# A three-part edit to a mixture-of-experts megakernel: an earlier weight load, unwaited scatters, and spare rows cleared in other pieces

## What is computed

```python
x = x + _layernorm(_L0_attn_ref(_layernorm(x), ...))   # softmax attention, 16 heads of 16, causal
x = x + _layernorm(_L0_ffn_ref(_layernorm(x), ...))    # one 256x256 product
x = x + _layernorm(_L1_attn_ref(_layernorm(x), ...))   # linear attention, gelu feed-forward
x = x + _layernorm(_L1_ffn_ref(_layernorm(x), ...))    # 8 experts, top 2, capacity 2151
```

```python
probs = softmax(xf @ Wg); topv, topi = top_k(probs, 2); gates = topv / sum(topv)
pos   = running count of each expert's tokens; keep = pos < cap
buf   = zeros(e * cap + 1, d).at[dest].set(repeat(xf, 2))
h     = gelu(buf[e] @ W1[e] + b1[e]);  y = h @ W2[e] + b2[e]
out   = sum over a token's two experts of gate * y (0 where it was not kept)
```

## Time and profile before

| what | us |
|---|---|
| median of 3 runs (4597.26 to 4608.24) | 4602.2 |
| the profiled execution, its own time | 4610.1 |
| its span, first to last instruction | 4608.3 |
| softmax block, about | 0 to 1473 |
| linear block, about | 1473 to 3637 |
| experts block, about | 3637 to 4535 |
| combine block, about | 4535 to 4608 |

### The profile page before, as it was taken

How to read it: one execution, slowest core, us unless ns; L and a number is a source line. 1 busy time by engine, 2 the same in 40 slices (tenths; PEclk the granted TensorE clock), 3 DMA queues, 4 the chain that set the end, 5 groups by cost and what they waited for, 6 DMA issues and landing times. The chain is left out here.

```text
span 4608.3 us, 78285 instructions
## 1 busy us (share of the span) xinstructions
PE 4088.1 (89%) x26868; PEld 3115.5 (68%) x26868; DVE 2812.6 (61%) x8170; ACT 1910.7 (41%) x3047; POOL 1191.9 (26%) x1096
## 2 busy tenths in 40 slices
PE   4999999999993899999999999999999599989990
PEld 2344444444442788888888888888888498989890
DVE  4787777887862665555565655555655455556554
ACT  1565666666662333343243333332332233333322
POOL 3243333433422211111111111111111133333334
PEclk8899989999985999999999999999999699999995
DMA  3442443353322000000000000000000133333335
GB/s 71 84 88 54 76 100 55 73 112 76 54 51 90 4 17 14 19 19 15 14 15 16 15 13 13 15 13 4 13 13 9 62 60 63 64 61 67 61 65 200
DMA packets 168272, 222.45 MB, mean 48 GB/s; under 512 B 26732, under 2 KB 143435, under 8 KB 167872
## 3 DMA queue, kind: packets, MB, share of 16 engines
q1 hardware_dynamic: 139840, 180.74, 17.0%
q0 software_dynamic: 25728, 28.03, 4.0%
q10 hardware_dynamic: 2304, 8.39, 0.4%
HBM read 85.92 MB, written 86.65 MB: 37 GB/s over the span
## 5 line engine op out<-in xcount | busy, mean ns | idle before, releaser
L787 ACT ACTIVATE probs<-a_scores 128x1024 f32<-128x1024 f32 (+3 forms) x768 | 615.3, 811 | 376.9 <-PE a_scores L691 370.2
L948 DVE CUSTOM_DVE_ANT_0 a_scores<-a_scores,mask 128x384 f32<-128x384 f32 (+3 forms) x1024 | 482.1, 515 | 121.4 <-PE a_scores L677 115.4
L691 PEld LDWEIGHTS a_scores<-q_st,k_st 50*128 50x128 f32 x1536 | 151.4, 194 | 411.6 <-issue 282.0
L252 POOL TENSOR_TENSOR l_ln_rstd<-l_ln_ve,minus_half 128x4 f32<-128x4 f32 x80 | 84.0, 1050 | 1230.9 <-DVE l_ln_ve L225 1230.7
L691 PE MATMUL a_scores<-q_st,k_st 50*128 50x512 f32 (+3 forms) x1536 | 354.8, 460 | 33.5 <-issue 24.7
L951 DVE TENSOR_REDUCE mx<-a_scores 128x2 f32<-128x1024 f32 x256 | 311.0, 1224 | 118.0 <-PE a_scores L677 116.9
L711 PE MATMUL a_out<-probs,v_aug 128*32 128x512 f32 (+3 forms) x3072 | 352.1, 533 | 1.9 <-POOL probs L880 1.8
L677 PE MATMUL a_scores<-k_st,q_st 48*128 48x512 f32 (+3 forms) x1536 | 309.5, 401 | 45.8 <-ACT probs L787 28.1
L2377 POOL DMA_INDIRECT expert_sums_scratch<-e_y,e_number x136 | 224.0, 1647 | 376.2 <-DMA expert_sums_scratch<-e_y,e_number 325.9
L880 POOL TENSOR_SCALAR_AFFINE_SELECT probs<-probs 128x512 f32<-128x512 f32 x256 | 162.6, 636 | 567.1 <-ACT probs L787 563.6
L2308 PE MATMUL e_out<-e_weights_lo,e_hT_hi 128*128 128x256 f32 x1088 | 308.4, 283 | 0.0
(11 more groups left out here) (259 smaller groups left out, 10228.6 us busy)
## 6 DMA issues: line engine op xcount, KB each, us to landing
q_st<-parts SPq DMA_DIRECT2D x192, 128.0 KB, 4.5
k_st<-parts SPq DMA_DIRECT2D x192, 128.0 KB, 6.2
expert_rows_scratch<-empty_row SPq DMA_DIRECT2D x8, 2210.0 KB, 14.3
e_weights<-in_L_ffn_W_dram SPq DMA_DIRECT2D x16, 1024.0 KB, 7.7
e_rows<-expert_rows_scratch SPq DMA_DIRECT2D x24, 390.0 KB
e_rows<-expert_rows_scratch SPq DMA_DIRECT2D x16, 520.0 KB
x_in<-in_L_attn_x_dram SPq DMA_DIRECT2D x8, 1024.0 KB, 6.9
expert_sums_scratch<-empty_row SPq DMA_DIRECT2D x8, 1024.0 KB, 15.9
```

The costliest lines, as they stand in the source:

```text
L691: last = nc.tensor.matmul(psum_r[:, R.slot(u), h2, 0:w], k_st[rows, 2 * hg + pair, i * P:(i + 1) * P], q_st[rows, 2 * hg + pair, q0:q0 + w ...
L787: nc.scalar.activation(probs[:, k % 3, 2 * pair:2 * pair + 2, 0:w], psum_r[:, R.slot(u), :, 0:w], ACT.Exp).then_inc(R.evacuated[R.slot(u)], 1)
L948: last = nc.vector.tensor_tensor_reduce(s, s, mask[:, HALF - w:HALF], 1.0, LEAST, ALU.add, ALU.max, out[:, h2, :])
```

## The change

Three parts, in one edit:

1. **Four sets of spare rows, and one wait for a group's scatters.** The sums get SPARE x 128 = 512 spare rows. The cleared rows carry N + 128 k + p, k being the tile's number modulo 4, so the tiles of one group (at most four in a row) never name the same spare row. POOL issues all scatters of a group and waits once. The rows are cleared in pieces of four tiles (532 KB), four in a turn and two more after the first.
2. **The first expert's weights are loaded in the linear block**, in its last group, once the last QK product is full. `e_weights` is now allocated first, over the place of the linear layer's `l_w_qkv_lo`. In the experts block the rows are issued ahead of the biases.
3. **The spare rows of the sums are zeroed after the first turn**, with the two extra pieces, and no longer at the softmax block's end.

```diff
-    sums_dram = nc.dram_tensor("expert_sums_scratch", (N + P, D), F32).ap()
+    sums_dram = nc.dram_tensor("expert_sums_scratch", (N + SPARE * P, D), F32).ap()
...
-                zv = rows_dram.rearrange("(e b p) d -> b p e d", p=P, e=SLOTS // P // B)
+                FOURS = SLOTS // P // SPARE
+                PER = FOURS // B
+                zv = rows_dram.rearrange("(f q p) d -> f p q d", p=P, q=SPARE)
+                fours = empty[:, :, :]
...
                 def clear_rows(b):
-                    sp.dma_start(zv[bass.ds(b, 1), :, :, :].rearrange("a p e d -> p (a e) d"),
-                                 empty[:, :].rearrange("p (a d) -> p a d", a=1).broadcast_to(
-                                     [P, SLOTS // P // B, RW])).then_inc(zeroed, 16)
+                    for f in range(PER):
+                        sp.dma_start(zv[bass.ds(b * PER + f, 1), :, :, :].rearrange("a p q d -> p (a q) d"),
+                                     fours).then_inc(zeroed, 16)
...
                 turn(0, GU_FIRST, True, False, True)
+                for f in range(B * PER, FOURS):
+                    sp.dma_start(zv[f], fours).then_inc(zeroed, 16)
+                sp.dma_start(sums_dram[N:N + SPARE * P, :].rearrange("(q p) d -> p q d", p=P),
+                             empty[:, :, 0:D]).then_inc(zeroed, 16)
...
                 sp.wait_ge(x2_stored, B * 16)
-                sp.dma_start(sums_dram[N:N + P, :], empty[:, 0:D]).then_inc(zeroed, 16)
-                sp.wait_ge(zeroed, 16 * (2 * B + 1))
+                sp.wait_ge(zeroed, 16 * (B + FOURS + 1))
...
                     store(g - 1, 1 - s)
+                    if last:
+
+                        G.wait_full(sp, g, U["QK"] + NQK - 1)
+                        load_weights(sp, W1, W2, 0, raw_e, e_loaded)
...
-                load_weights(0)
                 turns(sp, turn)
...
-                        if q % NGR == 0:
-
+                        def biases():
...
+                        if q % NGR == 0:
+                            biases()
...
-                                in_=y[:, q % 2, j, :], in_offset=None, bounds_check=N + P - 1,
+                                in_=y[:, q % 2, j, :], in_offset=None, bounds_check=N + SPARE * P - 1,
                                 compute_op=ALU.add).then_inc(added, 16)
 
-                            pool.wait_ge(added, i * (2 * CT * 16) + (e2 * CT + t0 + j + 1) * 16)
-                            pool.sem_inc(begun, 1)
+                        pool.wait_ge(added, i * (2 * CT * 16) + (e2 * CT + t0 + n) * 16)
                         pool.sem_inc(y_gone, 1)
```

More of the change, by code:

```diff
@@ L53 @@
 HELD = 6
+NW = 2 * CD * HE // HALF
+SPARE = 4
 class Ring:
@@ L142, in build, with load_weights @@
                           weight, disha, x2_dram, rows_dram, sums_dram)
+        with ExitStack() as ctx:
+            held = ctx.enter_context(nc.sbuf_tensor("x3_held", [P, HELD, G4, D], F32))
+            raw = ctx.enter_context(nc.sbuf_tensor("e_weights", [P, NW, HALF], F32))
+        raw_loaded = [whole.enter_context(nc.semaphore(name)) for name in ("e_w1_loaded", "e_w2_loaded")]
         linear_layer(nc, ident, minus_half, spot, x2_dram, g1, be1, Wq, Wk, Wv, Wo, g2, be2, Wf1, Wf2, Wg,
-                     x3_dram, rows_dram)
-        held = sb("x3_held", [P, HELD, G4, D])
-        experts(nc, ident, rows_dram, W1, b1, W2, b2, sums_dram, x3_dram, held)
+                     x3_dram, rows_dram, W1, W2, raw, raw_loaded)
+        sb("x3_held_place", [P, HELD, G4, D])
+        sb("e_weights_place", [P, NW, HALF])
+        experts(nc, ident, rows_dram, raw, raw_loaded, W1, b1, W2, b2, sums_dram, x3_dram, held)
         combine(nc, minus_half, sums_dram, x3_dram, held, out_rows)
+def load_weights(sp, W1, W2, e, raw, raw_loaded):
+    for n, w in enumerate((W1, W2)):
+        sp.dma_start(raw[:, n * (NW // 2):(n + 1) * (NW // 2), :].rearrange("p k n -> p (k n)"),
+                     w[bass.ds(e, 1), :, :].rearrange("a (c p) n -> p (a c) n", p=P)
+                     ).then_inc(raw_loaded[n], 16)
 def token_rows(dram):
@@ L333, in softmax_layer @@
         rden = sb("rden", [P, 4, 4, 1])
-        empty = sb("empty_row", [P, RW])
+        empty = sb("empty_row", [P, SPARE, RW])
         load = sem("a_weights_loaded")
@@ L372, in _ @@
                 nc.vector.memset(v_aug[:, :, :], 0.0).then_inc(filled, 1)
-                nc.vector.memset(empty[:, 0:D], 0.0).then_inc(filled, 1)
-                nc.vector.memset(empty[:, D + 1:RW], 0.0).then_inc(filled, 1)
-                nc.vector.tensor_scalar(empty[:, NUMBER:NUMBER + 1], spot[:, 0:1], float(N), None,
+                nc.vector.memset(empty[:, :, 0:D], 0.0).then_inc(filled, 1)
+                nc.vector.memset(empty[:, :, D + 1:RW], 0.0).then_inc(filled, 1)
+                assert SPARE == G4
+                nc.vector.tensor_scalar(empty[:, :, NUMBER], spot[:, :], float(N), None,
                                         ALU.add).then_inc(filled, 1)
@@ L559, in clear_rows @@
                 def clear_rows(b):
-                    sp.dma_start(zv[bass.ds(b, 1), :, :, :].rearrange("a p e d -> p (a e) d"),
-                                 empty[:, :].rearrange("p (a d) -> p a d", a=1).broadcast_to(
-                                     [P, SLOTS // P // B, RW])).then_inc(zeroed, 16)
+                    for f in range(PER):
+                        sp.dma_start(zv[bass.ds(b * PER + f, 1), :, :, :].rearrange("a p q d -> p (a q) d"),
+                                     fours).then_inc(zeroed, 16)
                     sp.dma_start(of_batch(sv, b),
-                                 empty[:, 0:D].rearrange("p (a d) -> p a d", a=1).broadcast_to(
+                                 empty[:, 0, 0:D].rearrange("p (a d) -> p a d", a=1).broadcast_to(
                                      [P, TT, D])).then_inc(zeroed, 16)
@@ L1112, in linear_layer @@
 def linear_layer(nc, ident, minus_half, spot, x2_dram, g1, be1, Wq, Wk, Wv, Wo, g2, be2, Wf1, Wf2, Wg,
-                 x3_dram, rows_dram):
+                 x3_dram, rows_dram, W1, W2, raw_e, e_loaded):
     NP = H1 // 2
@@ L2092, in _, with experts @@
                     locate(NGR - 1, step)
-def experts(nc, ident, rows_dram, W1, b1, W2, b2, sums_dram, x3_dram, held):
+def experts(nc, ident, rows_dram, raw, raw_loaded, W1, b1, W2, b2, sums_dram, x3_dram, held):
     MH = HE // P
@@ L2107, in experts @@
     NQ = 2 * NGR
-    NW = 2 * CD * HE // HALF
     PAIRS = (("hi", "hi"), ("hi", "lo"), ("lo", "hi"))
@@ L2140, in experts @@
         psum_y = ctx.enter_context(nc.psum_tensor("e_out", [P, 2, HALF], F32))
-        raw = sb("e_weights", [P, NW, HALF])
         w = {part: sb(f"e_weights_{part}", [P, 2, NW, HALF], F32R) for part in ("hi", "lo")}
@@ L2164, in experts @@
         YU = Ring(sem, "e_out", 2, NQ * 2)
-        raw_loaded = [sem("e_w1_loaded"), sem("e_w2_loaded")]
         b_loaded = [sem(f"e_biases_loaded{i}") for i in range(2)]
@@ L2219, in _ @@
                 rv = rows_dram.rearrange("(e t p) d -> e p t d", p=P, t=CT)
-                def load_weights(e):
-                    sp.dma_start(raw[:, 0:NW // 2, :].rearrange("p k n -> p (k n)"),
-                                 of_expert(W1, e, "a (c p) n -> p (a c) n", p=P)
-                                 ).then_inc(raw_loaded[0], 16)
-                    sp.dma_start(raw[:, NW // 2:NW, :].rearrange("p k n -> p (k n)"),
-                                 of_expert(W2, e, "a (c p) n -> p (a c) n", p=P)
-                                 ).then_inc(raw_loaded[1], 16)
                 def turn(i, seq, more):
@@ L2255, in turn @@
                                        count(i, seq, ("W", 1, NW - 1)))
-                            load_weights(e + 1)
-                load_weights(0)
+                            load_weights(sp, W1, W2, e + 1, raw, raw_loaded)
                 turns(sp, turn)
```

## The result

On the chip that timed both, the changed kernel took 4574.7 us (median of 6, 4566.8 to 4585.0), the kernel before 4607.5 us (median of 6, 4597.3 to 4611.9). The ratio is **0.9931, 95% interval 0.9913 to 0.9949**, so 32 us less with 23 to 40 as bounds. Timed again later, it was 0.9925 (0.9904 to 0.9946).

What follows compares the result with a forecast made beforehand. PE bounds the linear layer, untouched by the change; gains come only from gaps at the borders. The terms 2.0 + 5.8 + 4.2 + 20.6 = 32.6 us, off the 4602.2 median, gave 4569.6 us, range 4561 to 4584.

Steps and rivals of the forecast that it cites:

- A, spare rows' DMA: Softmax block's end: without the DMA clearing the spare rows, its issue and landing go; 2.0 us (1.5 to 2.2).
- B, experts' start: Start of the experts: early weights and rows ahead of biases bring PE's second turning forward; 5.8 us (3.5 to 7).
- C, turn ends: Turn ends among the experts: DVE no longer waits for POOL before the next turn's splits; 4.2 us (2 to 5.5).
- D, end: From PE's last product to the combine block's first load: POOL no longer a group behind; 20.6 us (16 to 21.5).
- the first rival: Scatters serve one after another in the DMA engines, so only issue overlaps; end gain 16.1 us, time 4574; chance 0.12.
- two paths, rows (5.4) and weights (6.2): Experts' start: PE's second turning follows group 1's rows (5.4 us earlier) or the next weights' issue (6.2 us earlier).
- the second rival: POOL did not hold the turn ends; group 1's rows still stand behind 2 MB of weights; time 4576.6, chance 0.10.
- The clearing: Softmax block: clearing the rows in pieces costs nothing, as up to 10 us of slack remain before the maxima's copy.
- the third rival: Softmax block: clearing pieces run one after another and delay the maxima; 72 us lost, time 4641.6; chance 0.04.
- The 11.6 us forecast for four pieces: Clearing in the softmax block: four pieces at 2.9 us each make 11.6 us, against 14.3 for the one DMA.
- A longer linear block: Sign against the prediction: a longer linear block would make it wrong; the early load there was taken to cost nothing.
- The fourth rival: An inner wait stays in some form or another engine holds the border; some 6 us remain, time 4596; chance 0.03.

## Why the prediction was right

| term | forecast | by the stretches | shown by |
|---|---|---|---|
| A, spare rows' DMA | 2.0 | 1.75 | put back: 3.0 lost, with 4 times the bytes |
| B, experts' start | 5.8 | 6.75 | late load: 6.4 lost; biases first: 0 |
| C, turn ends | 4.2 | 4.4 (5.8 by PE's waits) | waits back: 2.7 lost by PE's waits; the rest not shown |
| D, end | 20.6 | 20.4 | waits back: 21.0 lost |
| sum | 32.6 | 33.3 | ratio: 32, 23 to 40 |

The forecast median of 4569.6 lies 5.1 us below the measured 4574.7 because the kernel before, timed again beside it, was 5.3 above the median shown; the difference of 32.6 is what held. That it comes so close to 32 is in part luck: the measurement leaves 23 to 40, term B was 1 us too small, term C by PE's waits 1.6, and the kernel with the waits put back came out at 0.9997, with the 0.998 that terms A and B alone would give at the edge of its interval.

**Term D** came out step by step. The inner period is 1.86 us, as taken from the row scatters. The last landing is not later with three in flight, which rejects the first rival: it asked for 4519.5 - 4501.15 = 18.4 us of gap, 14.05 were measured. The argument from the engines' share, 1.13 us of all sixteen for each scatter, held.

**Term B** was right in mechanism, and undersized by 1 us. I gave two paths, rows (5.4) and weights (6.2), and took a value between them. The runs show that the weights' path alone decides: in all of the kernels with one row buffer that I looked at, the second turning comes 10.4 to 10.6 us after the next weights' issue, and when the biases went first, group 0's rows 1.3 us and group 1's 1.9 us later against the scatter, it did not move. The weights' issue itself came 9.98 us after the last scatter, where it had been 16.71, 6.7 us less. The step that was off is the time at which the splits begin. They took 3631.14 - 3625.33 = 5.8 us from the first cast, close to my 5.9, but the first cast came 4.2 us after the last scatter (3636.8 on the scale of before), where I had put it at 3637.3. So the next weights went out 0.6 us earlier than forecast; the other 0.4 us are what I had given away by taking a value below the 6.2 of that path. (The rows of group 0 were turned 4.05 us after their issue and not 5.2, so the path by the rows was quicker than forecast as well.) Of the second rival ("the rows of group 1 still stand behind 2 MB of weights") the observation was true. It did not lower the gain, as the weights moved up by the same amount.

**Term C** I read from one turn end and scaled to the others by their waits: 0, 1.7 and 2.5 us. By PE's idle time it was 1.0, 2.4 and 2.4, in sum 5.8, over my upper bound of 5.5. Putting the waits back cost only 2.7 (2.8 in the later pair of profiles), so the size of the term is met and its cause is shown for about half of what PE waited less. The second rival had C at zero; with the waits put back PE waited longer in both profiles than in any of the eight without them, so it falls.

**The clearing** cost nothing that can be seen, which the third rival denied, and even 16 pieces a turn did not make PE wait. The 11.6 us forecast for four pieces came near, but not by its argument of 4 x 2.9: the pieces are in flight together, the first lands after 6.4 to 7.5 us and the others 1.2 to 2.6 us after one another. By the fit on the Trainium skill's page "DMA: Bandwidth & Descriptors", section "Anatomy of one DMA — SWDGE (gpsimd) path" (2 us for each DMA and the bytes at 436 GB/s; it was measured on DMAs that GpSimd issues, these are SP's), 16 pieces would take about 30 us longer than one if each waited for the last, an estimate. This case's traces do not agree: the issue of the sixteen took SP 8.2 us in all, and the last landed 13.2 to 14.3 us after the first issue, so their fixed part is not paid one after another where nobody waits in between. Nor do they agree with the 7 us that it gives for the one DMA of before, which landed after 14.3 with the sums' zeros in flight beside it.

**A longer linear block** was named as a sign of being wrong, and the changed kernel's profile has it 4.8 us longer. Its later profile has 2157.7, 1.6 us less than the kernel before, and the two profiles with the early load taken out have 2161.6 and 2164.8, so the load in the last group is not what lengthened it.

**The fourth rival** falls with POOL's rows at the end: three scatters 1.86 us apart, no wait between them.

## What to carry to other kernels

A wait for one's own DMA inside a loop costs its landing each time round (2.85 us here), and it is paid in full only where the engine has become the last one, so count it at the ends and turns of a stage and not by the engine's busy share. If a wait only guards against two transfers hitting the same place, give them different places: 384 spare rows bought some 24 us (21.0 at the end and 2.7 at the turn ends, by putting the waits back). And when a load has been moved out of the way, look at which transfer lands last now; here it was the next 2 MB in front of 0.5 MB of rows on the same queue, and 4 KB a partition for a second buffer, with the rows issued ahead of the weights and the gating ahead of the wait, gained nearly as much again as the change (31 to 32 us).

## What was not expected

The same softmax block took from 1449 to 1467 us in different executions, and the difference sits in stretches of some 50 us in which PE's granted clock is 0.81 to 0.83, a mean over its two levels of 2.4 and 1.2 GHz, instead of 0.98 or 0.99. Two single profiles therefore showed 43 us where the change is worth 32, and the one kernel that had lost 6.4 us at its start (late weights) looked faster than the changed one in its first profile. And a small DMA with a broadcast source, the second bias, holds SP's queue for 3.3 us when 2 MB stand in front of it, 0.4 us when not; in the kernel before this was charged to the biases in the timeline, but belonged to the weights.
